# Two-layer transformer block, one core: the attention products of the first and the last head group in two rows of five or six, over both PSUM rings

## The reference, cut to what matters

```python
xn = _layernorm(x)
x = x + _L0_attn_ref(xn, w_qkv, w_o) + _L0_ffn_ref(xn, ...)
# _L0_attn_ref: 32 query heads, 8 key and value heads, head size 16, 2 batches of 512 rows
scores = jnp.einsum('bhsd,bhtd->bhst', xq, keys) * scale     # xq, keys after rope
scores = jnp.where(causal, scores, -jnp.inf)
probs = jax.nn.softmax(scores, axis=-1)
out = jnp.einsum('bhst,bhtd->bhsd', probs, values)
# _L0_ffn_ref: w_eff = w * (su @ sv); d = silu(x @ gate_eff.T) * (x @ up_eff.T); d @ down_eff.T
```

## Time and profile before

| | us |
|---|---|
| median of 3 runs | 662.78 |
| lowest, highest | 661.72, 663.55 |
| profiled execution, its own time | 662.82 |
| its span, first to last instruction | 661.1 |
| TensorE busy | 653.2 (99%) |
| TensorE weight loads busy | 497.9 (75%) |
| VectorE busy | 415.6 (63%) |
| ScalarE busy | 287.4 (43%) |
| GpSimd busy | 242.6 (37%) |

### The profile page before, as it was taken

One profiled execution on the slowest core, in us unless ns is written; L12 is line 12 of the kernel. 1 busy time (PEld: TensorE's weight loads), 2 busy tenths in 40 slices (PEclk: granted clock), 3 DMA queues, 4 the chain that ended last, 5 costly groups with the idle time before them and its releaser, 6 DMA issues.

```text
span 661.1 us, 9992 instructions
## 1 busy us (share of the span) xinstructions
PE 653.2 (99%) x3486; PEld 497.9 (75%) x3486; DVE 415.6 (63%) x986; ACT 287.4 (43%) x558; POOL 242.6 (37%) x243
## 2 busy tenths in 40 slices
PE   8999999999999999999999999999999999999998
PEld 7887666666666666666787878888888888888886
DVE  6967877667777777672477665376565555646501
ACT  4333455455555554554344234254434444343321
POOL 3597333223323233322144638503234332323443
PEclk9999999999999999999999999999999999999999
DMA  9548323253223222021255500500010111112011
GB/s 292 142 130 214 96 80 111 79 133 102 83 62 83 79 79 78 18 85 45 81 186 156 200 26 8 155 1 33 32 33 33 63 33 33 32 33 79 11 55 63
DMA packets 23401, 55.17 MB, mean 83 GB/s; under 512 B 3860, under 2 KB 4344, under 8 KB 22296
## 3 DMA queue, kind: packets, MB, share of 16 engines
q1 hardware_dynamic: 22840, 54.41, 27.7%
q10 hardware_dynamic: 512, 0.13, 0.1%
HBM read 42.86 MB, written 11.54 MB: 82 GB/s over the span
## 4 chain that ended last, share of the span: by engine, by line
PE 95%; DVE 2%; issue 1%; ACT 1%; POOL 0%; DMA 0%; DVEq 0%; ACTq 0%
PE bank L52 26%; PE bank L53 24%; PE bank L54 24%; PE bank L1098 6%; PE bank L1129 6%; PE bank L1116 2%; PE bank L180 2%; PE bank L704 1%; PE bank L108 1%; PE bank L1105 1%; PE bank L344 1%; DVE bank L1045 1%; PE bank L1685 1%; DVE acc L1890 0%; DVE lr L141 0%
## 5 line engine op out<-in xcount | busy, mean ns | idle before, releaser
L1045 DVE CUSTOM_DVE_ANT_0 bank<-bank,mask 128x512 f32<-128x512 f32 (+3 forms) x256 | 118.2, 521 | 43.6 <-PE bank L1098 43.5
L217 POOL TENSOR_TENSOR up_w_lo<-up_w_eff,up_w_hi 128x512 fp32r<-128x512 f32 x50 | 67.0, 1346 | 104.4 <-ACT up_w_hi L213 104.4
L382 POOL TENSOR_TENSOR down_h_lo<-hidden,down_h_hi 128x512 fp32r<-128x512 f32 x50 | 66.1, 1323 | 88.4 <-ACT down_h_hi L377 88.4
L997 ACT ACTIVATE probs<-bank 128x512 f32<-128x512 f32 x160 | 84.7, 596 | 25.3 <-PE bank L1116 25.3
L52 PE MATMUL bank<-x0T_hi,up_w_hi 128*128 128x512 f32 x224 | 94.9, 424 | 0.0
L54 PE MATMUL bank<-x0T_lo,up_w_hi 128*128 128x512 f32 x224 | 88.5, 395 | 0.0
L53 PE MATMUL bank<-x0T_hi,up_w_lo 128*128 128x512 f32 x224 | 88.4, 395 | 0.0
L52 PE MATMUL bank<-down_w_hi,down_h_hi 128*128 128x512 f32 x200 | 78.5, 392 | 0.4 <-DVE bind_cols L1405 0.4
L53 PE MATMUL bank<-down_w_hi,down_h_lo 128*128 128x512 f32 x200 | 78.0, 390 | 0.0
L954 POOL TENSOR_SCALAR_AFFINE_SELECT probs<-probs 128x512 f32<-128x512 f32 x64 | 39.9, 635 | 100.6 <-ACT probs L997 100.4
L377 ACT ACTIVATE down_h_hi<-hidden 128x512 fp32r<-128x512 f32 x50 | 31.6, 631 | 91.3 <-PE bank L54 91.3
(11 more groups left out here) (167 smaller groups left out, 1393.2 us busy)
## 6 DMA issues: line engine op xcount, KB each, us to landing
w_raw<-in_w_gate_up SPq DMA_DIRECT2D x25, 512.0 KB, 3.4
w_raw<-in_w_down SPq DMA_DIRECT2D x25, 256.0 KB, 2.9
q_stack<-q_hi SPq DMA_DIRECT2D x32, 128.0 KB, 3.3
att<-att_T SPq DMA_DIRECT2D x16, 256.0 KB, 2.0
q_hi<-rope_hi SPq DMA_DIRECT2D x8, 256.0 KB
q_lo<-rope_lo SPq DMA_DIRECT2D x8, 256.0 KB
q_stack<-q_lo SPq DMA_DIRECT2D x16, 128.0 KB, 3.4
attention_or_xn<-att SPq DMA_DIRECT2D x16, 128.0 KB
```

The lines of the kernel that those rows point to most:

```text
L217: pool.tensor_tensor(self.half(self.w_lo[:, o % 2], k), self.half(self.w_eff, k), f32(self.half(self.w_hi[:, o % 2], k)), ALU.subtract).th ...
L382: pool.tensor_tensor(self.h_lo[:, k % 2, :], self.hid[:, o, b * S:(b + 1) * S], f32(self.h_hi[:, k % 2, :]), ALU.subtract).then_inc(self.h ...
L997: act.activation(pt[:, BLOCK_OF[KEY_PIECES[p]], :, :], narrow.bank(("keys", g, p))[:, :].rearrange("p (h s) -> p h s", h=REP), ACT.Exp).th ...
L1045: dve.tensor_tensor_reduce(out=own, in0=own, in1=e.mask[:, S - w:S], scale=1.0, scalar=NEG, op0=ALU.add, op1=ALU.max, accum_out=rmax[:, i ...
```

## The change

In group 0 the 11 maxima pieces are dealt to two bursts, six to burst 0 and five to burst 2; bursts 1 and 3 have none (burst 3 keeps its transpose). In group 15 the ten key pieces are dealt as five to burst 64 and five to burst 66; bursts 65 and 67 are empty. So that six products can be issued in a row, the odd maxima pieces of group 0 go to `narrow`, and the key pieces 1, 3, 4, 6 and 8 of group 15 to `wide`; the low rows of group 15 go to `narrow`. All other groups keep their order. The order of each engine's queue follows the same tables, so VectorE's maxima and ScalarE's exponentials are gathered too.

```diff
+FIRST_MAX_BURST, LAST_KEY_BURST = [(0, 6), (0, 0), (6, 11), (0, 0)], [(0, 5), (0, 0), (5, 10), (0, 0)]
...
+        def max_pieces(g, at):
+            return range(*(FIRST_MAX_BURST if g == 0 else MAX_BURST)[at])
+        def key_pieces(g, at):
+            return range(*(LAST_KEY_BURST if g == GROUPS - 1 else KEY_BURST)[at])
+        def max_ring(g, p):
+            return narrow if g == 0 and p % 2 else wide
+        def key_ring(g, p):
+            return wide if g == GROUPS - 1 and p in (1, 3, 4, 6, 8) else narrow
+        def row_ring(g, half):
+            return narrow if half or g == GROUPS - 1 else wide
...
-                    for p in range(*MAX_BURST[s["at"]]):
-                        wide.place(("maxima", s["maxima"], p), reduced, NJ * REP * s["maxima"] + MAX_END[p])
+                    for p in max_pieces(s["maxima"], s["at"]):
+                        max_ring(s["maxima"], p).place(("maxima", s["maxima"], p), reduced, NJ * REP * s["maxima"] + MAX_END[p])
...
-                    for p in range(*KEY_BURST[s["at"]]):
-                        narrow.place(("keys", s["keys"], p), exp_done, KEYS * s["keys"] + p + 1)
+                    for p in key_pieces(s["keys"], s["at"]):
+                        key_ring(s["keys"], p).place(("keys", s["keys"], p), exp_done, KEYS * s["keys"] + p + 1)
...
-                    wide.place(("minus_max", s["low"], 0), neg_copied, 2 * s["low"] + 2)
-
-        row_ring = [wide, narrow]
+                    row_ring(s["low"], 0).place(("minus_max", s["low"], 0), neg_copied, 2 * s["low"] + 2)
...
-                    first, count = MAX_BURST[s["at"]][0], max(b - a for a, b in (MAX_BURST[s["at"]], KEY_BURST[s["at"]]))
-                    for n in range(count):
-                        if s["maxima"] is not None and first + n < MAX_BURST[s["at"]][1]:
-                            max_scores(s["maxima"], first + n)
-                        if s["keys"] is not None and KEY_BURST[s["at"]][0] + n < KEY_BURST[s["at"]][1]:
-                            key_scores(s["keys"], KEY_BURST[s["at"]][0] + n)
+                    maxima = list(max_pieces(s["maxima"], s["at"])) if s["maxima"] is not None else []
+                    keys = list(key_pieces(s["keys"], s["at"])) if s["keys"] is not None else []
+                    for n in range(max(len(maxima), len(keys))):
+                        if n < len(maxima):
+                            max_scores(s["maxima"], maxima[n])
+                        if n < len(keys):
+                            key_scores(s["keys"], keys[n])
```

More of the change, by code:

```diff
@@ L869, in attention_stage @@
                 if s["maxima"] is not None:
-                    for p in range(*MAX_BURST[s["at"]]):
-                        wide.place(("maxima", s["maxima"], p), reduced, NJ * REP * s["maxima"] + MAX_END[p])
+                    for p in max_pieces(s["maxima"], s["at"]):
+                        max_ring(s["maxima"], p).place(("maxima", s["maxima"], p), reduced, NJ * REP * s["maxima"] + MAX_END[p])
                 if s["keys"] is not None:
-                    for p in range(*KEY_BURST[s["at"]]):
-                        narrow.place(("keys", s["keys"], p), exp_done, KEYS * s["keys"] + p + 1)
+                    for p in key_pieces(s["keys"], s["at"]):
+                        key_ring(s["keys"], p).place(("keys", s["keys"], p), exp_done, KEYS * s["keys"] + p + 1)
                 if s["high"] is not None:
-                    narrow.place(("minus_max", s["high"], 1), neg_copied, 2 * s["high"] + 1)
+                    row_ring(s["high"], 1).place(("minus_max", s["high"], 1), neg_copied, 2 * s["high"] + 1)
                 if s["low"] is not None:
-                    wide.place(("minus_max", s["low"], 0), neg_copied, 2 * s["low"] + 2)
-        row_ring = [wide, narrow]
+                    row_ring(s["low"], 0).place(("minus_max", s["low"], 0), neg_copied, 2 * s["low"] + 2)
         def load_stack(sp, g):
@@ L977, in minus_max_row @@
                     act.wait_ge(neg_row[2 * half + 1], 16 * g)
-                act.activation(negrow[:, half, :], row_ring[half].bank(("minus_max", g, half))[0:2 * REP, 0:P],
+                act.activation(negrow[:, half, :], row_ring(g, half).bank(("minus_max", g, half))[0:2 * REP, 0:P],
                                ACT.Copy).then_inc(neg_copied, 1)
@@ L997, in exp_piece @@
                 act.activation(pt[:, BLOCK_OF[KEY_PIECES[p]], :, :],
-                               narrow.bank(("keys", g, p))[:, :].rearrange("p (h s) -> p h s", h=REP),
+                               key_ring(g, p).bank(("keys", g, p))[:, :].rearrange("p (h s) -> p h s", h=REP),
                                ACT.Exp).then_inc(exp_done, 1)
@@ L1042, in maxima @@
                 for n in range(nh):
-                    own = wide.bank(("maxima", g, p))[:, n * w:(n + 1) * w]
+                    own = max_ring(g, p).bank(("maxima", g, p))[:, n * w:(n + 1) * w]
                     dve.tensor_tensor_reduce(out=own, in0=own,
@@ L1093, in max_scores @@
                 i, h, nh = MAX_PIECES[p]
-                wide.free(pe, ("maxima", g, p))
+                max_ring(g, p).free(pe, ("maxima", g, p))
                 w = (i + 1) * P
-                bank = wide.bank(("maxima", g, p))
+                bank = max_ring(g, p).bank(("maxima", g, p))
                 for n in range(nh):
@@ L1103, in minus_max @@
                 pe.wait_ge(neg_done, 2 * g + 2 - half)
-                row_ring[half].free(pe, ("minus_max", g, half))
-                pe.transpose(row_ring[half].bank(("minus_max", g, half))[0:2 * REP, 0:P],
+                row_ring(g, half).free(pe, ("minus_max", g, half))
+                pe.transpose(row_ring(g, half).bank(("minus_max", g, half))[0:2 * REP, 0:P],
                              negm[:, half].rearrange("p i h -> p (i h)"), e.ident[:, :]).then_inc(neg_mm, 1)
@@ L1113, in key_scores @@
                     pe.wait_ge(neg_row[i], 16 * (g + 1))
-                narrow.free(pe, ("keys", g, p))
+                key_ring(g, p).free(pe, ("keys", g, p))
                 K = slice(r, r + STK)
-                pe.matmul(narrow.bank(("keys", g, p))[:, :], kst[K, slot, j * P:(j + 1) * P], qst[K, slot, :, i * P:(i + 1) * P],
+                pe.matmul(key_ring(g, p).bank(("keys", g, p))[:, :], kst[K, slot, j * P:(j + 1) * P], qst[K, slot, :, i * P:(i + 1) * P],
                           start=True, stop=True).then_inc(s2_mm, 1)
```

## The result

| | before | changed |
|---|---|---|
| median, us | 662.62 (13 runs, 661.72 to 663.55) | 663.95 (13 runs, 662.80 to 664.48) |
| ratio | | 1.0023, 95% interval 1.0016 to 1.0030 |
| profiled execution, us | 662.82 | 662.80 |
| its span, us | 661.1 | 661.1 |
| mean granted clock, run by run | 1.000 in the profiled one, 0.999 or 1.000 in each run of the experiments below | 0.997 in 12 of 13 runs, 1.000 in the profiled one |

The change costs 0.23%. The profiled execution doesn't show it: it is the one of the thirteen whose clock stayed at 1.000, the shortest of them, and it took as long as the profile before. So there are two questions: why this execution gained nothing where 0.18 us were forecast, and what the other twelve did. (The ratios are those on record with their intervals; they are not the quotients of the two medians and differ from them by up to 0.0004.

The account below looks back on a forecast made before the run. TensorE was taken to bound the kernel (95% of the wait chain), with VectorE deciding in the first group. Last group -0.76 and first group +0.58 gave -0.18 on 662.82, so 662.6 us, range 661.5 to 663.6.

Parts of the forecast that it names:

- Last group, TensorE: Group 15, bursts 65 and 67 gone: two ways in and out at 0.38 us each, 0.76 us saved.
- ring wait: Group 15, keys of bursts 64 and 66: their banks are free in time in both rings, no cost.
- the rows: Group 15: both low rows in by 307.8, before burst 66's keys need them; no cost, 0.6 us to spare.
- First group, VectorE's queue: Group 0: negation starts at 67.29, gate ends at 68.05, step 16's weights load at 68.17, 1.32 us later.
- First group, TensorE: Group 0: held for negation and gate until 68.17; low transpose at 71.36 instead of 70.78, 0.58 us lost.
- the wait at the low transpose: Group 0: TensorE's earlier stop of 0.71 us there is absorbed by the later start.
- rival (c): Group 0, burst 3: a stop of about 1.8 us lowers TensorE's clock, 4.2 us more, 666.8 us; chance 0.04.
- (a): Group 0: with both rings VectorE never holds TensorE, first group gains too; -2.12, 660.7 us; chance 0.12.
- Faster, same, slower: Whole kernel, with 0.3% (2.0 us) counted as no change: chances 0.04 faster, 0.92 same, 0.04 slower.

Follow-up runs that it names:

- run 1: Changed kernel with group 0's maxima dealt and placed as before, only group 15's keys gathered: 661.61 us, 0.68 under the kernel before, ratio 0.9990.
- run 3: The changed kernel itself, measured once more beside the kernel before: 663.48 us, ratio 1.0018.
- run 2: Changed kernel with group 15's keys as before, only group 0's maxima gathered: 664.34 us, 2.05 over the kernel before, ratio 1.0033.
- run 5: Kernel before, with three chained memsets on VectorE ahead of group 0's high negation: 664.69 us, 2.16 over the kernel before, ratio 1.0033.
- run 4: Kernel before, with five chained memsets on VectorE ahead of group 0's high negation: 666.45 us, 4.16 over the kernel before, ratio 1.0064.
- run 6: Changed kernel with 18 identity products on TensorE before its wait for group 0's high negation: 663.50 us, ratio 1.0021 to the kernel before.
- run 7: Changed kernel with 12 identity products on TensorE before its wait for group 0's high negation: 662.43 us, ratio 1.0002 to the kernel before.
- run 11: Changed kernel, split at step 14, group 0 dealt 6, 0, 2, 3, its low rows in the narrow ring: 660.65 us, ratio 0.9970 to the kernel before.
- run 9: Changed kernel with the split at step 14 and group 0 dealt 6, 0, 2, 3: 660.77 us, ratio 0.9976 to the kernel before.
- run 8: Changed kernel with VectorE's split of line 141 moved from step 10 to step 14: 660.87 us, ratio 0.9981 to the kernel before.
- run 10: Kernel before, with group 15's keys gathered and the split moved to step 14: 661.54 us, 0.77 under the kernel before, ratio 0.9988.

## Why the prediction was wrong

- *Last group, TensorE: right.* Two bursts at 0.38 us, 0.76; the trace shows 0.79, run 1 measures 0.68. No ring wait, and the rows weren't late: the exponentials took 2.55 us for five, the row DMAs went out at 305.80, the keys of burst 66 followed at 308.25 in one piece. (Half of 1.08 is 0.54, and the prediction counted 0.49 for an exponential; it changes no order.)
- *First group, VectorE's queue: one term mis-sized.* I used "split at 61.14, next piece 2.39 later". The 2.36 us of the row were not the length of the work but an end: 0.81 us after GpSimd's subtraction (60.98 to 63.37 before, 60.96 to 63.34 after). Started 0.6 us earlier, it took 0.6 longer. The piece behind it came at 64.19, not 63.53; 0.17 of these 0.66 us came back in the small maxima. So the negation came at 67.78, not 67.29, and step 16 loaded its weights at 68.65, not 68.17. The 0.58 us lost became 1.08 (71.86 against 70.78), so the sum should have been +0.29 where it said -0.18. The three runs of run 3 whose clock stayed up have a median of 0.35 over the kernel before; the profiled execution has -0.02, nearer to the forecast by 0.3 us that nothing here explains. The row was there to be seen: the later splits of the same shape take 0.95.
- *First group, TensorE: right in kind.* The stop was 2.0 + 0.4 us where I had 1.8; the wait at the low transpose was absorbed, as forecast.
- *The clock: the step that failed.* The sum has no term for it, and the range leaves it out. It stood there as rival (c), with a chance of 0.04: "around the present stop the granted clock stays at 1.00", taken from a stop of 0.7 us for one of 1.8. It is what happened in 20 of 24 runs, and it is most of the loss: 1.1 us between the medians of run 3 with and without the fall. Its price in the rival was too high: I charged 4.2 us for six steps, but the fall in runs 2 and 3 lasted 3.4 us, and one cost 0.9 us (run 5's median: 2.16 over, less 1.22 for the stop) to 1.7 (run 4), in the profiles 1.2 (run 3) to 2.1 (run 4). The Trainium skill, TensorE: Matmul & The Clock Gate, section HAM oscillation, says that idle gaps of the matrix engine bring the clock down. Runs 2 to 7 agree, though the gaps here are shorter than those that the page speaks of.
- *(a), more banks free TensorE: refuted for this order.* In the two stretches no matmul of the changed kernel waits for a bank; both waits are for VectorE's data. The stop of 0.7 us before was for a bank, though: the low transpose came behind the combination in `wide`. In run 11, which gives these rows to the other ring, the 0.50 us of that kind that run 9 still has is gone.
- *Faster, same, slower.* The measured 663.95 lies 0.35 us above the top of my range. The +1.3 us are inside the 0.3% that I called no change; but with 13 runs on each side the interval excludes no change, and the bound of 2.0 us that I set was far coarser than the measurement.

## What to carry to other kernels

When two engines work side by side, the length of an instruction in the trace may be a wait for another engine: compare it with the same shape elsewhere before moving it in a sum. A stop of TensorE that grows from 0.7 to 2 us must be priced twice, once for itself and once for the clock after it; where the stop can't be removed, keeping TensorE busy through it took the second price away. And gathering products into fewer rows pays where TensorE is alone the bound (0.7 us here for two rows), while in front of a VectorE queue it puts them ahead of what TensorE waits for next.

## What the hardware showed

- **The clock after a stop.** Stops of 1.5 + 0.4, 2.0 + 0.4 and 2.8 + 0.3 us in front of otherwise dense work were followed by the 1.2 GHz level in 35 of 40 runs (20 of 24 of the changed kernel, all 5 of run 2, all 5 of run 4, 5 of 6 of run 5). Stops of 0.5 to 0.8 us, and of 0.44 + 0.41, were not followed by it in any of 111 runs (68 of the kernel before, the others of runs 1, 8, 9 and 10), nor was one of 1.04 us ahead of 14.22 us in run 1's profile. In the four profiles with the fall the clock went down 3.5, 1.9, 1.4 and 2.0 us after TensorE had begun to stand (runs 2, 3, 4 and 5): in run 2 only at 68.6, 0.8 us after step 16 had begun, in run 4 in the middle of the stop. It stayed down for 3.4 us in three of them and for 6.8 in run 4's. What decides between a run with and one without the fall, and where it begins, stays open. In every profile TensorE also stands some 2.8 us before its first matmul, and the clock is at 1.00 afterwards; what it did ahead of the span isn't in the trace.
- **VectorE beside GpSimd.** The split reads two tensors from SBUF. In the nine profiles that have it at step 10 it began during GpSimd's subtraction and ended 0.81 to 0.82 us after that one's end (2.36 to 2.98 us long); alone it takes 0.95 (run 8). In the same stretch the maxima and the hidden product, which read one operand from PSUM, kept their lengths. The Trainium skill, GPSIMD Engine Reference, section Specifications, says that GpSimd's way to SBUF is shared with VectorE, with contention for VectorE instructions that have two SBUF inputs; the runs agree, and the end that stays put, whether the split began 0.24 or 0.84 us into GpSimd's instruction, shows a wait for that instruction and not a slower pace.
- **Scatter.** In the profiles, the first maxima on VectorE start anywhere from 55.7 to 57.0 us, with nothing changed ahead of them. The two profiles compared at the top both start late, at 56.9, so their comparison is fair, but neither is a typical run.
